# The second stage's projection steps on TensorE, issued in four pieces between the attention's products

## The chip, the cores and the metric

The kernel runs on one core of one Trainium2 chip. The core has five engines that run their own instruction streams and meet at semaphores: TensorE (PE in the rows; PEld is its weight load), VectorE (DVE), ScalarE (ACT), GpSimd (POOL) and SyncE (SP), which issues the DMAs. The metric is the time on the device in microseconds (us), the median of several runs.

## The reference, cut to what matters

Two transformer layers over four batches of 512 tokens of width 256. The change concerns the end of the first layer's attention and the projections of the second layer:

```
xn = layernorm(x)
# layer 0: 16 heads of 16
scores = einsum('bhqd,bhkd->bhqk', q, k) * scale
attn = einsum('bhqk,bhkd->bhqd', softmax(scores), v)
combined = g * mem_out / denom + (1 - g) * attn
x = x + combined @ Wo.T + ffn0(xn)
# layer 1
xn = layernorm(x)
q, k, v = silu(xn @ Wq), silu(xn @ Wk), silu(xn @ Wv)
gate = (xn @ Wg1) @ Wg2
logits = xn @ w_router          # two experts of eight per token
```

What follows (the linear attention of layer 1, its experts and the sum) is the third stage.

## The kernel before, in words

There are three stages, with a barrier between them. The first normalises, projects q, k, v of layer 0 and runs its experts; the second, the function `middle`, does the softmax attention of layer 0 and, beside it, the projections of layer 1; the third does the rest.

The second stage goes through four batches, each in four groups of four heads, each group in four tiles of 128 keys: sixteen tiles a batch, here 0 to 15, which the code calls slots. In one tile TensorE makes, for each of the four heads h, a score product (line 1219, into `psE`, two buffers in turn) and a row product (line 1201, into `psM`, two buffers in turn). The score products are of the present group; ScalarE turns each into probabilities with an exponential (line 1006). The row products are of the group after the next; VectorE takes from each the negated maximum of a row (line 1075), which the scores of that group will need. Then `values` (line 1228) multiplies the four heads' probabilities of the tile before with v, four matmuls of 32 output rows. Once in a group, in its second tile, four small transposes (line 1208) turn the maxima of the next group; VectorE copies them (line 1098) and two DMAs bring them into place.

Beside the attention of batch n + 1 run the steps of batch n, each in a fixed tile and, on every engine, after that engine's own attention work of the tile (`beside`). On TensorE: heads 0 to 3 in tiles 0 to 3 (lines 1267, 1270), the transposes of the combined heads in 4, the output projection in 5, the transposes of x in 8, the first half projection (q) in 9, the router's logits and the low-rank gate input in 10, its transposes in 11, the second half (k) in 12, the gate in 13, k by tokens in 14 and v by tokens in 15. The other engines' steps between them: VectorE combines the terms (`weigh_terms`, 0 to 3), adds the residual, normalises (7), splits x into a high and a low part (8), chooses the experts (10); ScalarE copies (4, 8) and applies Silu or a sigmoid (9, 12 to 15), for which it loads another activation table and then the exponential's again; GpSimd adds the terms. A TensorE step waits at its first matmul for the other engine's step on its input, and hands on at its last matmul. The first batch has nothing beside it; the last batch's own steps come at the end, alone.

All instructions of an engine run in the order in which they are written; semaphores make them wait. In `attend` that order, within a tile, is: two scores, (the turned maxima,) two rows, the values of the tile before, two scores, the whole step, two rows.

Of the kernel before, what the change touches and what calls it, by code (L numbers as in the profile page):

```python
# [732 lines left out]
RW = E + HD  # L733
# [3 lines left out]
def middle(nc, io, scratch, keep):  # L737
# [8 lines left out]
    with ExitStack() as ctx:  # L746
# [12 lines left out]
        ident, identb = sb("ident", [P, P]), sb("identb", [P, P], BF16)  # L759
# [67 lines left out]
        STORES, PARTS = 16 * STORES1, 16 * PARTS1  # L827
        SLOTS = GROUPS * TILES

        def loop(eng, attend, steps, ready=lambda: None):  # L830


            def batch(b, beside, last):
                for g in range(GROUPS):
                    attend(b, g, last, lambda k: [step(beside) for step in steps.get(TILES * g + k, ()) if beside is not None])

            batch(0, None, False)
            ready()
            with eng.Fori(0, BATCHES - 2) as b:
                batch(b + 1, b, False)  # L840
            batch(BATCHES - 1, BATCHES - 2, True)
            for slot in sorted(steps):
                for step in steps[slot]:
                    step(BATCHES - 1)
# [349 lines left out]
        def _(pe):  # L1194
# [17 lines left out]
            def attend(b, g, last, beside):  # L1212
# [20 lines left out]
                for k in range(TILES):  # L1233
                    ahead = not (last and g >= GROUPS - 2)
                    next_rows = G + 2, (g + 2) % GROUPS, k, b if g < 2 else b + 1
                    scores(k, (0, 1))
                    if k == 1 and not (last and g == GROUPS - 1):
                        turn_max(G + 1, (g + 1) % 2)
                    if ahead:
                        rows(*next_rows, (0, 1))  # L1240
                    if k:
                        values(k - 1)
                    scores(k, (2, 3))
                    beside(k)
                    if ahead:
                        rows(*next_rows, (2, 3))
                values(TILES - 1)


            def heads(t):  # L1250
                def step(n):

                    if t == 0:
                        pe.wait_ge(out_copied, GROUPS * (n + 1))
                        pe.wait_ge(qf_in, 16 * n + 16)
                        pe.wait_ge(v_done, n)
                    elif not alone(n):
                        pe.wait_ge(terms, TILES * n + t)
                    elif t == 1:
# [6 lines left out]
                    for g in range(GROUPS):  # L1266
                        nc.tensor.matmul(ps[:, 0, g * w:(g + 1) * w], outT[:, g, c], sel[:, :], start=True, stop=True,
                                         skip_group_check=True)
                    for k in range(KT):
# [3 lines left out]
                    mm.then_inc(heads_ps, 1)  # L1273
                return step

            def turn_combined(n):
                pe.wait_ge(combined_done, TILES * n + TILES)
                for t in range(TILES):
                    for k in range(KT):
                        mm = nc.tensor.transpose(psX[:, k, t * P:(t + 1) * P], combined[:, t, k * P:(k + 1) * P], ident[:, :])  # L1280
                mm.then_inc(combT_ps, 1)

            def project_out(n):
                pe.wait_ge(combT_done, n + 1)
                for t in range(TILES):
                    for k in range(KT):
                        mm = nc.tensor.matmul(psX[:, t // 2, t % 2 * D:(t % 2 + 1) * D], combT[:, k, t * P:(t + 1) * P], wo[:, k, :],
                                              start=k == 0, stop=k == KT - 1, skip_group_check=True)
                mm.then_inc(y_ps, 1)

            def turn_x(n):
                pe.wait_ge(norm.xn_done, TILES * n + TILES)
                for t in range(TILES):
                    for k in range(KT):
                        mm = nc.tensor.transpose(psX[:, k, t * P:(t + 1) * P], xn[:, t, k * P:(k + 1) * P], ident[:, :])
                mm.then_inc(xT_ps, 1)

            def project_half(i):
                def step(n):
                    if i == 0:  # L1300
                        pe.wait_ge(xlo, n + 1)
                    elif not alone(n):
                        pe.wait_ge(lowT_done, n + 1)
                        pe.wait_ge(routing.copied, n + 1)
                    else:
# [8 lines left out]
            def logits_low(n):  # L1314
                if not alone(n):
                    pe.wait_ge(half_done, 2 * n + 1)
                for t in range(TILES):
                    c = slice(t * P, (t + 1) * P)
                    mm = three(nc, second(n)[:, 0, t * RW:(t + 1) * RW],
                               [(xT[0][:, k, c], xT[1][:, k, c], wr[0][:, k, :], wr[1][:, k, :]) for k in range(KT)])  # L1320
                mm.then_inc(low_ps, 1)

            def turn_low(n):
                pe.wait_ge(low_done, n + 1)
                for t in range(TILES):
                    mm = nc.tensor.transpose(second(n)[0:HD, 1, t * P:(t + 1) * P], low[:, t, :], ident[:, :])
                mm.then_inc(lowT_ps, 1)

            def project_gate(n):
                pe.wait_ge(lowT_done, n + 1)  # L1330
                pe.wait_ge(routing.copied, n + 1)
                if not alone(n):
                    pe.wait_ge(half_done, 2 * n + 2)
                for t in range(TILES):
                    mm = nc.tensor.matmul(second(n)[:, t // 2, (t % 2) * D:(t % 2 + 1) * D], lowT[:, t * P:(t + 1) * P],
                                          wg2[:, :], start=True, stop=True, skip_group_check=True)
                mm.then_inc(gate_ps, 1)

            def project_tokens(i, free, done):

                def step(n):
                    ps = second(n) if i else psX
                    if not alone(n):
                        pe.wait_ge(free, n + 1)
                    elif i:
                        pe.wait_ge(gate_done, n + 1)
                    else:
                        pe.wait_ge(half_done, 2 * n + 2)
                    for t in range(TILES):
                        c = slice(t * P, (t + 1) * P)  # L1350
                        mm = three(nc, ps[:, t // 2, (t % 2) * D:(t % 2 + 1) * D],
                                   [(xT[0][:, k, c], xT[1][:, k, c], wkv[0][:, k, i * D:(i + 1) * D], wkv[1][:, k, i * D:(i + 1) * D])
                                    for k in range(KT)])
                    mm.then_inc(done, 1)
                return step

            for t in range(TILES):
# [8 lines left out]
            def ready():  # L1366
# [694 lines left out]
```

## Time and profile before

| | us |
|---|---|
| median of 3 runs | 1190.88 (1188.92 to 1192.23) |
| profiled execution, span of its instructions | 1186.0 |
| second stage, first row product to the end of its last steps | 309 to about 730 |
| TensorE busy, share of the span | 972.0 (82%) |
| VectorE busy | 584.5 (49%) |
| ScalarE busy | 433.3 (37%) |
| GpSimd busy | 311.8 (26%) |

Times of the trace are counted from the span's start. The profile has no time of the profiled execution beyond its span; the runs' median is 4.9 us longer than that span. Matmuls are pipelined, so that the duration of one overlaps the next: distances from start to start tell what a group of matmuls costs. A granted clock of 1.00 is 2.4 GHz, 0.50 is 1.2 GHz, and a value between is the mean of a stretch that has both.

### The profile page before, as it was taken

Reading aid. Unit: us, or ns where it says so; the run is one execution under the profiler, and the core shown is the slowest. Engines: PE = TensorE matmul, PEld = TensorE weight load, DVE = VectorE, ACT = ScalarE, POOL = GpSimd, SP = SyncE. Lnnn points to the kernel's source line nnn. Section 1 sums busy time; section 2 is a strip of 40 time slices with the busy share of each in tenths; the row PEclk is TensorE's granted clock in tenths of the full one; section 3 lists DMA queues with packets and bytes.
Section 4 is the critical chain, followed back from the end, with each engine's and each line's share of the span. In section 5 each row is a group of like instructions: output and inputs, shape, how many; then the busy total and the mean of one; then the engine's idle time right before and its main releaser. Section 6 shows DMA issues by size and latency. Waiting matters only on the chain. (4 is left out here: it accounts for less than half of the span.)

```text
span 1186.0 us, 16176 instructions
## 1 busy us (share of the span) xinstructions
PE 972.0 (82%) x5323; PEld 623.9 (53%) x5323; DVE 584.5 (49%) x1221; ACT 433.3 (37%) x662; POOL 311.8 (26%) x217
## 2 busy tenths in 40 slices
PE   3699999999589999999998763259999888999871
PEld 2588888888112334444434552235556555665541
DVE  4556566643577785577573322533233333333335
ACT  3435354452245556647646513002222221222210
POOL 3622425153230002012002121033333333333210
PEclk9989999999679998899898877569999999999975
DMA  6713314240523222412321205994322232333352
GB/s 212 224 36 96 110 54 150 54 151 1 145 62 91 66 79 93 145 59 89 133 65 63 98 32 165 274 286 122 109 77 80 80 77 76 85 78 89 81 175 71
DMA packets 150413, 125.47 MB, mean 106 GB/s; under 512 B 63424, under 2 KB 128080, under 8 KB 150352
## 3 DMA queue, kind: packets, MB, share of 16 engines
q1 hardware_dynamic: 146608, 114.45, 32.4%
q0 software_dynamic: 3744, 10.23, 2.9%
q8 instruction: 36, 0.59, 0.2%
q14 instruction: 25, 0.20, 0.1%
HBM read 85.76 MB, written 38.86 MB: 105 GB/s over the span
## 5 line engine op out<-in xcount | busy, mean ns | idle before, releaser
L1075 DVE TENSOR_REDUCE b_negmax<-b_psM 128x1 f32<-128x512 f32 x256 | 163.2, 683 | 75.6 <-PE b_psM L1201 72.6
L1006 ACT ACTIVATE b_probs<-b_psE 128x512 f32<-128x512 f32 x256 | 138.8, 595 | 118.2 <-PE b_psE L1219 117.3
L1201 PE MATMUL b_psM<-b_kst,b_qst 96*128 96x512 bf16 x256 | 98.5, 432 | 27.6 <-DVE b_negmax L1075 13.7
L1219 PE MATMUL b_psE<-b_qst,b_kst 98*128 98x512 bf16 x256 | 89.8, 410 | 15.4 <-ACT b_probs L1006 10.8
L402 POOL TENSOR_TENSOR a_hh<-a_h,a_hh 128x512 fp32r<-128x512 f32 x44 | 57.7, 1312 | 145.5 <-ACT a_hh L455 145.5
L1580 POOL DMA_INDIRECT scratch_ys<-d_y,d_put x39 | 40.2, 1030 | 178.4 <-ACT d_y L1618 176.8
L1847 PE MATMUL d_psG<-d_w,d_xT 128*128 x156 | 80.7, 642 | 4.1 <-issue 3.2
L1855 PE MATMUL d_psU<-d_w,d_xT 128*128 x156 | 79.9, 638 | 0.0
L1219 PEld LDWEIGHTS b_psE<-b_qst,b_kst 98*128 98x128 bf16 x256 | 20.9, 99 | 107.4 <-ACT b_probs L1006 53.8
L1872 PE MATMUL d_psY<-d_w,d_hidden 128*128 x312 | 76.7, 390 | 0.3 <-ACT d_hidden L1612 0.3
L1228 PE MATMUL b_psV<-b_probs,b_vst 128*32 128x512 f32 x512 | 73.6, 648 | 3.2 <-ACT b_probs L1006 3.2
L1586 POOL TENSOR_TENSOR d_rs<-d_ss,d_neghalf 128x16 f32<-128x16 f32 x16 | 46.8, 2928 | 93.0 <-DVE d_ss L1762 93.0
L1201 PEld LDWEIGHTS b_psM<-b_kst,b_qst 96*128 96x128 bf16 x256 | 24.3, 100 | 84.0 <-DVE b_negmax L1075 60.5
L1872 PEld LDWEIGHTS d_psY<-d_w,d_hidden 128*128 128x128 f32 x312 | 58.7, 194 | 15.5 <-issue 8.9
L1732 DVE TENSOR_TENSOR d_probs<-d_ps,decay 128x512 f32<-128x512 f32 x64 | 43.2, 687 | 43.4 <-PE d_ps L1886 43.1
L528 DVE TENSOR_TENSOR a_h<-a_h,a_psG 128x512 f32<-128x512 f32 x44 | 30.2, 686 | 68.4 <-ACT a_h L452 68.4
L1618 ACT ACTIVATE d_y<-d_psY 128x256 f32<-128x256 f32 x39 | 14.9, 383 | 125.4 <-PE d_psY L1872 125.4
L1727 DVE TENSOR_TENSOR d_hidden<-d_hidden,d_psU 128x512 f32<-128x512 f32 x39 | 26.8, 687 | 67.2 <-PE d_psU L1855 67.0
L1931 PE MATMUL d_ps<-d_ident,d_normed 128*128 128x128 f32 x32 | 8.0, 337 | 61.6 <-DVE d_normed L1770 61.6
L1606 ACT ACTIVATE d_hidden<-d_psG 128x512 f32<-128x512 f32 x39 | 23.3, 597 | 94.2 <-PE d_psG L1847 94.2
L956 POOL TENSOR_TENSOR b_combined<-b_both 128x256 f32<-128x256 f32 x16 | 11.6, 724 | 167.6 <-DVE b_both L1119 167.6
L455 ACT ACTIVATE a_hh<-a_h 128x512 fp32r<-128x512 f32 x44 | 27.8, 632 | 73.7 <-DVE a_h L533 73.7
(310 smaller groups left out, 2174.7 us busy)
## 6 DMA issues: line engine op xcount, KB each, us to landing
scratch_parts<-a_part SPq DMA_DIRECT2D x12, 512.0 KB, 4.0
b_qst<-scratch_parts SPq DMA_DIRECT2D x96, 64.0 KB, 2.3
b_kst<-scratch_parts SPq DMA_DIRECT2D x96, 64.0 KB, 2.3
scratch_parts<-b_part SPq DMA_DIRECT2D x24, 256.0 KB, 3.4
d_qst<-scratch_parts SPq DMA_DIRECT2D x96, 64.0 KB, 2.7
d_kst<-scratch_parts SPq DMA_DIRECT2D x96, 64.0 KB, 2.9
a_cbc<-scratch_cT SPq DMA_DIRECT2D x16, 256.0 KB, 3.9
scratch_v<-a_v SPq DMA_DIRECT2D x4, 1024.0 KB, 4.3
```

The costliest lines, as they stand in the source:

```text
L402: nc.gpsimd.tensor_tensor(hh[s % HSLOTS][1][:, :], h[s % 2][:, :], hh[s % HSLOTS][0][:, :].bitcast(F32), ALU.subtract).then_inc(lo_done, 1)
L1006: nc.scalar.activation(probs[k % PSLOTS][:, h, :], psE[h % 2][:, :], ACT.Exp, scale=float(HD) ** -0.5).then_inc(scores_used[h % 2], 1)
L1075: nc.vector.tensor_reduce(negmax[i][:, t, h:h + 1], psM[:, h % 2, :], AX_X, ALU.max, negate=True).then_inc(rows_used[h % 2], 1)
L1201: nc.tensor.matmul(psM[:, h % 2, :], qst[g][0:STACK, h, t * P:(t + 1) * P], kst[g][0:STACK, h, :], start=True, stop=True).then_inc(rows_re ...
L1219: nc.tensor.matmul(psE[h % 2][:, :], kst[g][0:STACKM, h, k * P:(k + 1) * P], qst[g][0:STACKM, h, :], start=True, stop=True).then_inc(score ...
L1228: mm = nc.tensor.matmul(psV[VW * h:VW * (h + 1), :], vst[g][:, k, VW * h:VW * (h + 1)], probs[k % PSLOTS][:, h, :], start=k == 0, stop=k = ...
L1580: nc.gpsimd.indirect_dma_start(scratch["ys1"], bass.IndirectOffsetOnAxis(ap=put[:, b:b + 1], axis=0), y[b % YSLOTS][:, :], None).then_inc( ...
L1586: nc.gpsimd.tensor_tensor(rs[:, :], ss[:, :], neghalf[:, :], ALU.pow).then_inc(rs_done, 1)
L1732: nc.vector.tensor_tensor(probs[g][:, :], (ps1 if g % 2 else ps0)[:, :], decay[:, HG * g:HG * g + HG, :].rearrange("p h c -> p (h c)"), AL ...
L1847: mm = nc.tensor.matmul(psG[:, :], xT[b % 2][:, k, :], weights(b, GATE + k * H1, H1), start=k == 0, stop=k == KT - 1)
L1855: mm = nc.tensor.matmul(psU[:, :], xT[b % 2][:, k, :], weights(b, UP + k * H1, H1), start=k == 0, stop=k == KT - 1)
L1872: mm = nc.tensor.matmul(psY[:, 0:D], hT[b % 2][:, k, :], weights(b, DOWN + k * D, D), start=k == 0, stop=k == HT1 - 1)
```

## The change

Each of TensorE's steps is cut into four pieces of equal work (a quarter of its matmuls in the same order), and the four heads of a tile are no longer taken in pairs: behind the score of each head come its row product and then one piece of the step. The values of the tile before come behind the second piece. The waits of a step stand before its first piece, and its hand-over after its last piece, as they stood before its first and after its last matmul. The steps keep their tiles, and the other engines their order. In the batch at the end, without attention beside it, the pieces follow each other and the order is that of before.

```diff
                 for k in range(TILES):
                     ahead = not (last and g >= GROUPS - 2)
                     next_rows = G + 2, (g + 2) % GROUPS, k, b if g < 2 else b + 1
-                    scores(k, (0, 1))
-                    if k == 1 and not (last and g == GROUPS - 1):
-                        turn_max(G + 1, (g + 1) % 2)
-                    if ahead:
-                        rows(*next_rows, (0, 1))
-                    if k:
-                        values(k - 1)
-                    scores(k, (2, 3))
-                    beside(k)
-                    if ahead:
-                        rows(*next_rows, (2, 3))
+                    for h in range(HG):
+                        scores(k, (h,))
+                        if ahead:
+                            rows(*next_rows, (h,))
+                        if k == 1 and h == 0 and not (last and g == GROUPS - 1):
+                            turn_max(G + 1, (g + 1) % 2)
+                        beside(k, h)
+                        if k and h == 1:
+                            values(k - 1)
                 values(TILES - 1)
...
             def project_half(i):
-                def step(n):
-                    if i == 0:
+                def step(n, piece):
+                    if piece == 0 and i == 0:
                         pe.wait_ge(xlo, n + 1)
-                    elif not alone(n):
+                    elif piece == 0 and not alone(n):
                         pe.wait_ge(lowT_done, n + 1)
                         pe.wait_ge(routing.copied, n + 1)
-                    else:
+                    elif piece == 0:
                         pe.wait_ge(half_done, 2 * n + 1)
-                    for m in range(KT):
-                        c = slice((KT * i + m) * P, (KT * i + m + 1) * P)
-                        mm = three(nc, psX[:, m, :], [(wqk[0][:, k, c], wqk[1][:, k, c], xT[0][:, k, :], xT[1][:, k, :])
-                                                      for k in range(KT)])
-                    mm.then_inc(half_ps, 1)
+                    m, k = piece // KT, piece % KT
+                    c = slice((KT * i + m) * P, (KT * i + m + 1) * P)
+                    mm = three(nc, psX[:, m, :], [(wqk[0][:, k, c], wqk[1][:, k, c], xT[0][:, k, :], xT[1][:, k, :])],
+                               start=k == 0, last=k == KT - 1)
+                    if piece == KT * KT - 1:
+                        mm.then_inc(half_ps, 1)
                 return step
...
             loop(pe, attend, {0: (heads(0),), 1: (heads(1),), 2: (heads(2),), 3: (heads(3),), 4: (turn_combined,), 5: (project_out,),
                               8: (turn_x,), 9: (project_half(0),), 10: (logits_low,), 11: (turn_low,), 12: (project_half(1),),
                               13: (project_gate,), 14: (project_tokens(0, gate_done, kk_ps),),
-                              15: (project_tokens(1, kk_done, v_ps),)}, ready)
+                              15: (project_tokens(1, kk_done, v_ps),)}, ready, tuple((piece,) for piece in range(HG)))
```

On TensorE, a tile of the first batch, with nothing beside it (`b_psE` are scores, `b_psM` rows, `b_psV` values), before:

```order
L1219 MATMUL b_psE<-b_qst,b_kst 128x512 x2
L1201 MATMUL b_psM<-b_kst,b_qst 128x512 x2
L1228 MATMUL b_psV<-b_probs,b_vst 32x512 x4
L1219 MATMUL b_psE<-b_qst,b_kst 128x512 x2
L1201 MATMUL b_psM<-b_kst,b_qst 128x512 x2
```

and the same tile now:

```order
L1220 MATMUL b_psE<-b_qst,b_kst 128x512
L1202 MATMUL b_psM<-b_kst,b_qst 128x512
L1220 MATMUL b_psE<-b_qst,b_kst 128x512
L1202 MATMUL b_psM<-b_kst,b_qst 128x512
L1229 MATMUL b_psV<-b_probs,b_vst 32x512 x4
L1220 MATMUL b_psE<-b_qst,b_kst 128x512
L1202 MATMUL b_psM<-b_kst,b_qst 128x512
L1220 MATMUL b_psE<-b_qst,b_kst 128x512
L1202 MATMUL b_psM<-b_kst,b_qst 128x512
```

Each row product stands behind its own head's score. On TensorE, tile 2 with heads 2 beside it (`b_psX`, from `b_outT` and from `mem`), before:

```order
L1219 MATMUL b_psE<-b_qst,b_kst 128x512 x2
L1201 MATMUL b_psM<-b_kst,b_qst 128x512 x2
L1228 MATMUL b_psV<-b_probs,b_vst 32x512 x4
L1219 MATMUL b_psE<-b_qst,b_kst 128x512 x2
L1267 MATMUL b_psX<-b_sel,b_outT 128x68 x4
L1270 MATMUL b_psX<-mem,b_qf 128x136 x2
L1201 MATMUL b_psM<-b_kst,b_qst 128x512 x2
```

and the same tile now:

```order
L1220 MATMUL b_psE<-b_qst,b_kst 128x512
L1202 MATMUL b_psM<-b_kst,b_qst 128x512
L1267 MATMUL b_psX<-b_sel,b_outT 128x68 x2
L1220 MATMUL b_psE<-b_qst,b_kst 128x512
L1202 MATMUL b_psM<-b_kst,b_qst 128x512
L1267 MATMUL b_psX<-b_sel,b_outT 128x68 x2
L1229 MATMUL b_psV<-b_probs,b_vst 32x512 x4
L1220 MATMUL b_psE<-b_qst,b_kst 128x512
L1202 MATMUL b_psM<-b_kst,b_qst 128x512
L1271 MATMUL b_psX<-mem,b_qf 128x136
L1220 MATMUL b_psE<-b_qst,b_kst 128x512
L1202 MATMUL b_psM<-b_kst,b_qst 128x512
```

The step's first matmul moved from behind the fourth score to behind the first row, and its last from ahead of the third row to behind the fourth.

## Rows read from the trace of the kernel before

**Rows 1.** Waits, 330 to 700 us: who waited for whom, total us, times, longest

```profile
ACT b_probs L1006 <- PE b_psE L1219: 117.3, 74, 4.2
DVE b_negmax L1075 <- PE b_psM L1201: 72.6, 41, 4.5
```

**Rows 2.** Four batches: us, busy (x count) of each engine, granted clock, DMA share, GB/s

```profile
331.70:401.50 69.80, 60.78 (x291) 16.05 (x292) 52.94 (x86) 38.16 (x69) 4.87 (x3) 0.91 0.26 75
401.50:496.10 94.60, 87.61 (x461) 42.53 (x460) 62.28 (x135) 56.66 (x84) 12.66 (x9) 0.92 0.25 79
496.10:587.60 91.50, 84.76 (x461) 40.11 (x460) 62.97 (x135) 56.67 (x84) 12.66 (x9) 0.95 0.31 103
587.60:673.50 85.90, 75.24 (x406) 37.63 (x404) 40.70 (x95) 53.06 (x79) 12.63 (x9) 0.91 0.25 83
```

**Rows 3.** Order of time, first batch: start, us, engine, line, out<-in [idle before <-releaser]

```profile
378.76 1.07 PE L1228 MATMUL b_psV<-b_probs,b_vst 128*32 128x512 f32 x8
379.76 0.60 PE L1219 MATMUL b_psE<-b_qst,b_kst 98*128 98x512 bf16 x2
380.20 0.60 PE L1201 MATMUL b_psM<-b_kst,b_qst 96*128 96x512 bf16 x2
...
377.09 2.64 DVE L1075 TENSOR_REDUCE b_negmax<-b_psM 128x1 f32<-128x512 f32 x4 [0.89 <-PE b_psM L1201]
```

**Rows 4.** Order of time, TensorE, heads in tiles 1 and 2

```profile
404.82 1.01 PE L1267 MATMUL b_psX<-b_sel,b_outT 128*128 128x68 f32 x8
...
406.18 0.60 PE L1201 MATMUL b_psM<-b_kst,b_qst 96*128 96x512 bf16 x2
...
411.06 0.60 PE L1201 MATMUL b_psM<-b_kst,b_qst 96*128 96x512 bf16 x2
```

**Rows 5.** Order of time, VectorE, tile 1: reductions, combining, next reductions

```profile
406.60 1.29 DVE L1075 TENSOR_REDUCE b_negmax<-b_psM 128x1 f32<-128x512 f32 x2 [0.86 <-PE b_psM L1201]
407.81 0.35 DVE L1114 RECIPROCAL b_scale<-b_psX 128x32 f32<-128x32 f32 x1
...
409.02 1.28 DVE L1075 TENSOR_REDUCE b_negmax<-b_psM 128x1 f32<-128x512 f32 x2
```

**Rows 6.** Order of time, tiles 8 and 9: copy, split, half projection, rows

```profile
440.69 1.02 ACT L1017 ACTIVATE b_xT<-b_psX 128x1024 fp32r<-128x1024 f32 x1 [0.28 <-PE b_psX L1295]
442.68 1.20 DVE L1138 TENSOR_TENSOR b_xT<-b_psX,b_xT 128x1024 fp32r<-128x1024 f32 x1
443.94 0.19 PEld L58 LDWEIGHTS b_psX<-b_xT,b_wqk 128*128 128x128 f32 x1
443.96 0.59 PE L58 MATMUL b_psX<-b_xT,b_wqk 128*128 128x512 f32 x1
444.38 0.40 PE L59 MATMUL b_psX<-b_xT,b_wqk 128*128 128x512 f32 x1
...
446.89 0.61 PE L1201 MATMUL b_psM<-b_kst,b_qst 96*128 96x512 bf16 x2
```

**Rows 7.** Order of time, ScalarE, tile 9: table load and Silu

```profile
445.23 1.28 ACT L1023 ACT_TABLE_LOAD   x1
447.08 1.02 ACT L1023 ACTIVATE b_half<-b_psX 128x1024 f32<-128x1024 f32 x1 [0.57 <-PE b_psX L60]
```

**Rows 8.** Order of time, VectorE and TensorE at the turn of the batch

```profile
489.91 1.22 DVE L1158 TENSOR_TENSOR b_part<-b_half,b_part 128x1024 bf16<-128x1024 f32 x1
491.04 1.22 DVE L1142 TENSOR_TENSOR b_kd<-b_combT,b_kdec 128x1024 f32<-128x1024 f32 x1
...
492.48 0.69 DVE L1105 COPY b_outT<-b_psV 128x512 f32<-128x512 f32 x1
...
493.47 1.41 PE L1267 MATMUL b_psX<-b_sel,b_outT 128*128 128x68 f32 x8 [0.63 <-DVE b_outT L1105]
```

**Rows 9.** Stretches of 2 us, columns as in rows 2

```profile
366.00:368.00 2.00, 1.38 (x11) 0.31 (x11) 1.72 (x5) 0.62 (x2) 0.00 (x0) 1.00 0.04 13
...
454.00:456.00 2.00, 2.00 (x6) 0.51 (x4) 1.59 (x5) 0.85 (x2) 0.73 (x1) 0.50 0.00 0
...
586.00:588.00 2.00, 2.00 (x10) 1.39 (x9) 0.55 (x2) 0.00 (x0) 0.00 (x0) 0.56 0.47 142
```

More of the change, by code:

```diff
@@ L828, in middle, with loop @@
         SLOTS = GROUPS * TILES
-        def loop(eng, attend, steps, ready=lambda: None):
+        def loop(eng, attend, steps, ready=lambda: None, pieces=((),)):
             def batch(b, beside, last):
                 for g in range(GROUPS):
-                    attend(b, g, last, lambda k: [step(beside) for step in steps.get(TILES * g + k, ()) if beside is not None])
+                    attend(b, g, last, lambda k, *piece: [step(beside, *piece) for step in steps.get(TILES * g + k, ()) if beside is not None])
             batch(0, None, False)
@@ L843, in loop @@
                 for step in steps[slot]:
-                    step(BATCHES - 1)
+                    for piece in pieces:
+                        step(BATCHES - 1, *piece)
         def alone(n):
@@ L1265, in step @@
                     c, w = slice(t * P, (t + 1) * P), HG * (HD + 1)
[L1266 to L1269, printed above, removed]
+                    if piece < 2:
+                        for g in (2 * piece, 2 * piece + 1):
+                            nc.tensor.matmul(ps[:, 0, g * w:(g + 1) * w], outT[:, g, c], sel[:, :], start=True, stop=True,
+                                             skip_group_check=True)
+                    else:
+                        k = piece - 2
                         mm = nc.tensor.matmul(ps[:, 1, MW * k:MW * (k + 1)], qf[:, k, c],
@@ L1283, in project_out @@
[L1283 to L1296, printed above, removed]
+                        if k == KT - 1:
+                            mm.then_inc(heads_ps, 1)
@@ L1316, in logits_low @@
+                return step
+            def logits_low(n, t):
+                if t == 0 and not alone(n):
                     pe.wait_ge(half_done, 2 * n + 1)
-                for t in range(TILES):
-                    c = slice(t * P, (t + 1) * P)
[L1319 to L1354, printed above, removed]
+                c = slice(t * P, (t + 1) * P)
@@ new lines, in logits_low, with turn_low @@
+                mm = three(nc, second(n)[:, 0, t * RW:(t + 1) * RW],
+                           [(xT[0][:, k, c], xT[1][:, k, c], wr[0][:, k, :], wr[1][:, k, :]) for k in range(KT)])
+                if t == TILES - 1:
+                    mm.then_inc(low_ps, 1)
+            def turn_low(n, t):
+                if t == 0:
+                    pe.wait_ge(low_done, n + 1)
+                mm = nc.tensor.transpose(second(n)[0:HD, 1, t * P:(t + 1) * P], low[:, t, :], ident[:, :])
+                if t == TILES - 1:
+                    mm.then_inc(lowT_ps, 1)
@@ new lines, in project_gate @@
+            def project_gate(n, t):
+                if t == 0:
+                    pe.wait_ge(lowT_done, n + 1)
+                    pe.wait_ge(routing.copied, n + 1)
+                if t == 0 and not alone(n):
+                    pe.wait_ge(half_done, 2 * n + 2)
+                mm = nc.tensor.matmul(second(n)[:, t // 2, (t % 2) * D:(t % 2 + 1) * D], lowT[:, t * P:(t + 1) * P],
+                                      wg2[:, :], start=True, stop=True, skip_group_check=True)
+                if t == TILES - 1:
+                    mm.then_inc(gate_ps, 1)
@@ new lines, in project_tokens, with step @@
+            def project_tokens(i, free, done):
+                def step(n, t):
+                    ps = second(n) if i else psX
+                    if t == 0 and not alone(n):
+                        pe.wait_ge(free, n + 1)
+                    elif t == 0 and i:
+                        pe.wait_ge(gate_done, n + 1)
+                    elif t == 0:
+                        pe.wait_ge(half_done, 2 * n + 2)
+                    c = slice(t * P, (t + 1) * P)
+                    mm = three(nc, ps[:, t // 2, (t % 2) * D:(t % 2 + 1) * D],
+                               [(xT[0][:, k, c], xT[1][:, k, c], wkv[0][:, k, i * D:(i + 1) * D], wkv[1][:, k, i * D:(i + 1) * D])
+                                for k in range(KT)])
+                    if t == TILES - 1:
+                        mm.then_inc(done, 1)
```

41 lines of the change are left out of this document (27 added, 14 removed).

## The prediction

> **What bounds the kernel now.** I read the stretches of the second stage first, then its waits, then TensorE's, VectorE's and ScalarE's instructions in order of time in the batch that begins at 401.5 us. Name the products of one tile s (score), r (row), V (values) and b (the step beside); number the sixteen tiles of a batch 0 to 15; call the start of a tile's fourth row product its mark. From mark to mark the first batch, which has no step beside it, takes 69.8 us with its start-up, the next two 94.6 and 91.5, and the last, to the end of its values, 85.9 [rows 2]. In these three TensorE is busy 93, 93 and 88%, VectorE 66, 69 and 47%, ScalarE about 61%: TensorE's row of instructions is the path. ScalarE and VectorE wait for it, 117.3 us for scores and 72.6 us for rows [rows 1], because a whole step (1.36 us for heads, 2.93 us for a half projection) stands between two pairs of products [rows 4, 6].
>
> The granted clock is part of that length. 0.92, 0.95 and 0.91 are means of the two levels, so 2 x (1 - clock) x length = 15.1, 9.2 and 15.5 us pass at 1.2 GHz; at 2.4 GHz that work takes half. Without these stretches the three batches are 94.6 - 7.6 = 87.0, 91.5 - 4.6 = 86.9 and 85.9 - 7.7 = 78.2 us. The first two, which do the same work, agree to 0.1 us, so I hold the slow stretches to be on the path.
>
> **Batch 0: two products closer.** Here only the order of s, r and V changes. Before, VectorE does four reductions in 2.64 us and waits 0.89 us: a tile is 3.52 us [rows 3]. The limit is a ring: r1 waits for the reduction of r3 of the tile before, then V (1.0 us) and s2, s3 (0.44) come before r2. After, r2 and r3 have one score between them and s2 alone ahead: from a mark, the reduction of r3 ends at +1.2; r1 can start at +1.27, ends at +1.5, V at +2.5, s2, r2, s3 (0.22 each) at +3.16. That is 0.36 us less in two tiles of four; the second tile of a group gains 0.2 and the first 0.1 in the same way. 1.0 us a group, four groups: **-4.0 us**.
>
> **The steps: the wait comes 1.9 us sooner.** Each step waits, at its first matmul, for another engine's work on the step before, and that work is queued behind that engine's four exponentials or reductions of the tile before. Before, TensorE had r2, r3, s0, s1, r0, r1, V, s2, s3 (2.9 us) to issue in the meantime; now it has r3, b3, s0, r0. What stands behind the waiting matmul is everything TensorE has: s1 and r1, on which ScalarE and VectorE then run dry. So a tile becomes release + 3 pieces + s1, r1, V, s2, r2, s3 = release + 3 pieces + 2.1 us, from mark to mark, where the release is counted from the last mark.
>
> Tiles 2 and 3 (heads): r3's reduction starts 0.42 after the mark and ends at 1.03; the combining of the terms takes 1.21 us (407.81 to 409.02) [rows 5]; release 2.33 with the signal. A piece is 1.36 / 4 = 0.34. 2.33 + 1.05 + 2.1 = 5.48, before 4.88 [rows 4]. Tile 1 has the turned maxima and their copy ahead of the combining: 6.25. Three tiles: 17.2.
>
> Tiles 9, 10, 13, 14 and 15 wait for a ScalarE step. Tile 9: s3's exponential ends at 0.75, the copy of 1.02 us at 1.8, VectorE's split of 1.20 us at 3.05 [rows 6]. Tile 10: exponential 0.75, table load 1.28 us, Silu 1.02 us, 3.05 [rows 7]. The other three have the same load and a 1024-wide activation. TensorE reaches its wait at 1.1 to 1.35, so it stands about 1.8 us. A piece of 2.93 us less the 0.2 of its first load is 0.68 [rows 6]: 3.1 + 2.04 + 2.1 = 7.24, five tiles 36.2. (The gate's pieces are shorter and the token projections' longer; together they differ by 0.3.)
>
> Tile 0 of the next batch waits for the last copy of outT. VectorE has, behind r3's reduction at 1.03, two passes of 1.2 us, the split maxima and a copy of 0.69 us [rows 8]: release 4.45, three pieces, and s1, r1, s2, r2, s3 without V: 6.6 us. Before, TensorE waited there 0.63 us, with s2, s3, r0 and r1 already out.
>
> Tiles 4 to 8, 11 and 12, walked in the same way: 4.9 (GpSimd's sum of the terms is the release), 6.6, 3.72, 4.35, 4.78 (VectorE's normalisation is), 4.52 and 5.38. They sum to 34.3; VectorE's own work sets most of them, and the spread rows help it.
>
> A batch is 17.2 + 36.2 + 6.6 + 34.3 = 94.3 us at full clock, against 87.0 and 86.9: +7.3 and +7.4. In the last batch groups 2 and 3 have no rows, so a tile there is 0.44 us shorter (6.8 five times, 3.6, 3.25, 4.7, and 1.95 to the end of V: 47.5); with 17.2 and 19.6 for tiles 1 to 7 it is 84.3, against 78.2: +6.1. Together **+20.8 us**. The last batch's steps, done with nothing beside them, keep their order: 0.
>
> **The first weight load of a step.** The 0.19 us load of the half projection's first matmul begins at 443.94, just after the split's end at 443.88 [rows 6]: it starts behind its wait and not before, and the second matmul starts 0.42 us after the first, where a product of 512 columns takes 0.22. Most steps of before waited for nothing and paid little of it; now about eight in a batch do: 8 x 0.19 x 3 = **+4.6 us**, between 0 and this. The Trainium skill, in "TensorE: Matmul & The Clock Gate" (section "What a matmul computes"), says that weight loads are pulled ahead of running matmuls; were that so across the wait too, this term would be 0 and the sum 4.6 less. The row shows it otherwise.
>
> **The clock.** It falls to 0.50 after the narrow matmuls of the logits (454 to 456), and to 0.56 behind the pauses at the turn of a batch (586 to 588) [rows 9]. The change removes long narrow stretches, since the logits come in quarters, and adds pauses. No row shows both together. Bounds: all 39.8 us of slow stretches go, -19.9 us; or they double, +19.9 us. I take the number of today, 0 change, midway between the two and nearest to the rows.
>
> **Sum.** -4.0 + 20.8 + 4.6 = +21.4 us on the profiled execution, whose span is 1186.0 us: 1207.4. The runs' median of 1190.88 is 4.9 above that span, so **1212 us**, with 1200 to 1226 as its own range (the load term 0, two microseconds either way in each batch's walk, and some of the clock).
>
> **Rivals.**
> *More pauses, more time at 1.2 GHz.* The slow stretches double: 1212 + 19.9 = 1232 us. For it: about nine waits in a batch of 1.3 to 2 us, and the pauses at the turn of a batch were followed by a fall [rows 9]. Against it: at 366 to 368, in the first batch, TensorE was busy 1.38 of 2 us, and the clock stayed at 1.00 [rows 9]. The Trainium skill has this as a rule ("TensorE: Matmul & The Clock Gate", section "A second HAM failure mode: psum-queue depth-cycling"): short idle moments between groups of matmuls let the clock swing between its levels. The row at 586 agrees; the row at 366 does not.
>
> *The clock stays up.* With the logits in quarters no slow stretch is left: 1212 - 19.9 = 1192 us, no measurable change. For it: the longest falls follow logits and gate. Against it: the pause at each of these steps.
>
> *The waits are covered, and it is faster.* If the releasing steps end before TensorE comes to the first piece, the batch is TensorE's work: 5.5 us in place of 7.24 in five tiles, 4.3 in place of 5.7 in three, 3.2 in place of 6.6 at the turn of the batch, some 15 us less than 94.3, or 8 less than 87. Three batches and the first: about -24 - 4, 1163 us. It decides at the first piece: 21.4 us over 27 waits (nine a batch) is 0.8 each, so where the waits average under 1.0 us instead of 1.8 the change is not slower. For it: VectorE and ScalarE wait 190 us for TensorE, and both are fed more evenly. Against it: s3's exponential, an activation of 1.02 us and a table load all follow the fourth score, and only 1.1 to 1.35 us of TensorE's work cover them.
>
> **How the numbers follow.** Forecast 0.56, more slow clock 0.20, clock stays up 0.12, covered 0.12. About 0.3% (3.6 us) is what a measurement of this kernel tells from no change. Covered is faster; the case at 1192 I split into 0.03 faster, 0.05 same, 0.04 slower; the rest is slower: 0.15, 0.05, 0.80. The range goes from 1190, which takes in the case of the steady clock, to 1236; it leaves out the covered case and the worst clock.
>
> **What would show it.** Waits of TensorE's first piece, in the half and token projections for ScalarE or VectorE, of 1.5 to 2 us each; the heads' matmuls waiting over 1 us for the combining; batches of 94 to 101 us; a first batch 4 us shorter, its VectorE waiting less for rows. Wrong would be: these waits under 1 us, batches under 90 us, or a mean clock above 0.97 in the three.

## The result, and the profile after

The change made the kernel slower: 1241.44 us (median of 4 runs, 1239.57 to 1242.45) against 1191.56 us for the kernel before, run beside it, a ratio of 1.041 with a 95% interval of 1.0388 to 1.0433. The forecast was 1212 us with a range up to 1236: the direction was right, the size too small by 29 us.

First where the time went. The same stretches as in [rows 2], from mark to mark, in the kernel after; in front of them the first batch from its first row product to the first heads matmul, 87.04 us, where before the same stretch is 91.03 us. Columns as in [rows 2]. The first batch before:

```profile
308.87:399.90 91.03, 78.52 (x315) 18.12 (x315) 73.82 (x121) 46.54 (x93) 9.36 (x4) 0.81 0.34 96
```

After:

```profile
312.38:399.42 87.04, 76.65 (x311) 18.25 (x311) 71.30 (x120) 45.73 (x90) 9.34 (x4) 0.80 0.33 97
...
402.30:512.80 110.50, 91.78 (x462) 46.10 (x460) 67.27 (x136) 59.43 (x85) 12.66 (x9) 0.87 0.23 70
512.80:626.40 113.60, 96.24 (x462) 46.84 (x460) 65.52 (x136) 59.30 (x84) 12.67 (x9) 0.82 0.25 82
626.40:725.60 99.20, 81.29 (x404) 40.20 (x402) 41.90 (x94) 54.14 (x78) 12.65 (x9) 0.84 0.21 71
```

The three batches are 110.50, 113.60 and 99.20 us against 94.60, 91.50 and 85.90: +51.3 us. The granted clock, next to last but two, fell to 0.87, 0.82 and 0.84. Worked as in the prediction, 2 x (1 - clock) x length, 28.7, 40.9 and 31.7 us passed at 1.2 GHz, 101.3 us in place of 39.8. Half of the difference is 30.8 us; what is left, 20.5 us, is length at full clock: 96.1, 93.2 and 83.3 us against 87.0, 86.9 and 78.2. The span as a whole grew by 54.7 us (1186.0 to 1240.7): counted from heads to heads the three batches give +53.0, the first batch -4.0, the first stage +3.5 (its end moved from 308.87 to 312.38, with no change in its code) and all behind the batches +2.2. The medians grew by less, 49.9 us. In every run that lists both, the time is 1.75 to 1.85 us above the span (1242.45 and 1240.7 here), so the profiled execution of before was nearly 4 us faster than its median, and that of after 1 us slower than its own.

Who waits now. First for TensorE, as in [rows 1], over 330 to 760 us (the batches are longer); then TensorE's own waits between 395 and 690 us, before and after (the last batch ends at 674 us before and at 727 after, so that the list of after lacks a third of it). Columns: who waited for whom, total us, times, longest.

```profile
ACT b_probs L1007 <- PE b_psE L1220: 176.3, 148, 4.2
DVE b_negmax L1076 <- PE b_psM L1202: 101.0, 87, 3.3
```

Before:

```profile
PE b_psE L1219 <- ACT b_probs L1006: 10.8, 11, 1.6
PE b_psM L1201 <- DVE b_negmax L1075: 7.0, 28, 0.6
PE b_psX L1280 <- POOL b_combined L956: 3.2, 4, 2.4
PE b_psX L1267 <- DVE b_outT L1105: 1.4, 2, 0.8
```

After:

```profile
PE b_psX L1267 <- DVE b_both L1120: 13.3, 9, 1.8
PE b_psX L58 <- DVE b_xT L1139: 5.5, 3, 2.1
PE b_psX L58 <- ACT b_half L1024: 5.4, 3, 2.1
PE b_psX L1267 <- DVE b_outT L1106: 4.1, 3, 1.9
...
PE b_psX L58 <- ACT b_sg L1042: 3.4, 2, 1.9
PE b_psX L58 <- ACT b_combT L1047: 3.3, 2, 1.6
```

ScalarE waited 117.3 us for scores before and waits 176.3 now, VectorE 72.6 and now 101.0: both starve behind a TensorE that stands at the first piece of a step. Those waits (`b_psX`) were nearly absent before. In the three whole batches of after, the nine tiles that the prediction named have 27 of them, 43 us together: 0.45 us at the very first and 1.3 to 2.2 us at the other 26.

One of them from near by: TensorE in order of time, tiles 1 and 2 with heads beside them (start, us, engine, line, out<-in, and in brackets the idle time before and what ended it).

```profile
404.76 0.81 PE L1267 MATMUL b_psX<-b_sel,b_outT 128*128 128x68 f32 x4 [1.79 <-DVE b_both L1120]
405.36 0.64 PE L1220 MATMUL b_psE<-b_qst,b_kst 98*128 98x512 bf16 x1
405.79 0.64 PE L1202 MATMUL b_psM<-b_kst,b_qst 96*128 96x512 bf16 x1
406.21 0.96 PE L1267 MATMUL b_psX<-b_sel,b_outT 128*128 128x68 f32 x4
...
409.69 0.38 PE L1202 MATMUL b_psM<-b_kst,b_qst 96*128 96x512 bf16 x1
...
412.07 0.66 PE L1267 MATMUL b_psX<-b_sel,b_outT 128*128 128x68 f32 x4 [1.33 <-DVE b_both L1120]
412.57 0.38 PE L1220 MATMUL b_psE<-b_qst,b_kst 98*128 98x512 bf16 x1
412.79 0.38 PE L1202 MATMUL b_psM<-b_kst,b_qst 96*128 96x512 bf16 x1
...
415.39 0.38 PE L1202 MATMUL b_psM<-b_kst,b_qst 96*128 96x512 bf16 x1
```

From mark (409.69) to mark (415.39) tile 2 takes 5.70 us, where the prediction's walk through the tile had 5.48, and its release comes 2.38 us after the mark, where the walk had 2.33. That is the wait's own price. The other price stands in the lines behind 404.76: after the wait of 1.79 us a score and its row are 0.43 us apart (405.36 to 405.79), after the wait of 1.33 us 0.22 (412.57 to 412.79). The granted clock beside it, in stretches of 2 us, columns as before:

```profile
406.00:408.00 2.00, 2.00 (x13) 1.09 (x12) 0.69 (x1) 0.60 (x1) 0.00 (x0) 0.50 0.52 138
...
412.00:414.00 2.00, 1.93 (x18) 1.36 (x18) 1.31 (x3) 0.60 (x1) 0.72 (x1) 1.00 0.00 0
...
450.00:452.00 2.00, 2.00 (x7) 1.18 (x5) 0.64 (x1) 0.60 (x1) 0.00 (x0) 0.50 0.56 166
...
488.00:490.00 2.00, 1.78 (x7) 1.53 (x8) 0.78 (x2) 1.97 (x3) 0.00 (x1) 0.50 0.46 159
...
508.00:510.00 2.00, 2.00 (x9) 1.53 (x9) 0.69 (x1) 0.60 (x1) 0.00 (x0) 0.50 0.44 130
```

At 450, 488 and 508 it is the same: 0.50 right behind a first piece that waited, 1.70 us at the half projection, 1.93 at the token projection, 1.91 at the turn of the batch.

Over the three batches of after the trace has 15 separate stretches at 0.50. Fourteen begin within 2.5 us of the end of one of the 26 long waits, and one (at 487.1 us) inside the wait that ends at 488.22. Of the other 11 waits three end in a stretch that was already at 0.50, and eight bring no fall, such as that of 1.33 us at 412.07.

### The profile page after: what moved, and what is told of

Read it like the earlier page. It is cut to its first block and busy times, and to the rows that moved or that the text cites. A ratio compares the mean times of both kernels' runs of the same rounds, so it can differ in the third digit from the quotient of the medians.

```text
span 1240.7 us, 16176 instructions
## 1 busy us (share of the span) xinstructions
PE 997.2 (80%) x5323; PEld 642.7 (52%) x5323; DVE 593.5 (48%) x1221; ACT 441.7 (36%) x662; POOL 311.8 (25%) x217
## 5 line engine op out<-in xcount | busy, mean ns | idle before, releaser
L1076 DVE TENSOR_REDUCE b_negmax<-b_psM 128x1 f32<-128x512 f32 x256 | 167.5, 685 | 103.1 <-PE b_psM L1202 101.0
L1007 ACT ACTIVATE b_probs<-b_psE 128x512 f32<-128x512 f32 x256 | 148.5, 597 | 178.9 <-PE b_psE L1220 176.3
L1202 PE MATMUL b_psM<-b_kst,b_qst 96*128 96x512 bf16 x256 | 114.0, 447 | 22.0 <-DMA b_vst<-scratch_v 11.3
L1220 PE MATMUL b_psE<-b_qst,b_kst 98*128 98x512 bf16 x256 | 110.2, 431 | 0.5
L1229 PE MATMUL b_psV<-b_probs,b_vst 128*32 128x512 f32 x512 | 82.0, 716 | 5.8 <-ACT b_probs L1007 5.6
L1220 PEld LDWEIGHTS b_psE<-b_qst,b_kst 98*128 98x128 bf16 x256 | 27.1, 106 | 88.9 <-issue 75.9
L455 ACT ACTIVATE a_hh<-a_h 128x512 fp32r<-128x512 f32 x44 | 27.8, 633 | 73.7 <-DVE a_h L533 73.7
```

What stands on the lines that cost most here:

```text
L1007: nc.scalar.activation(probs[k % PSLOTS][:, h, :], psE[h % 2][:, :], ACT.Exp, scale=float(HD) ** -0.5).then_inc(scores_used[h % 2], 1)
L1076: nc.vector.tensor_reduce(negmax[i][:, t, h:h + 1], psM[:, h % 2, :], AX_X, ALU.max, negate=True).then_inc(rows_used[h % 2], 1)
L1202: nc.tensor.matmul(psM[:, h % 2, :], qst[g][0:STACK, h, t * P:(t + 1) * P], kst[g][0:STACK, h, :], start=True, stop=True).then_inc(rows_re ...
L1220: nc.tensor.matmul(psE[h % 2][:, :], kst[g][0:STACKM, h, k * P:(k + 1) * P], qst[g][0:STACKM, h, :], start=True, stop=True).then_inc(score ...
L1229: mm = nc.tensor.matmul(psV[VW * h:VW * (h + 1), :], vst[g][:, k, VW * h:VW * (h + 1)], probs[k % PSLOTS][:, h, :], start=k == 0, stop=k = ...
```

## The experiments

In each profile I measured the three batches with a step beside them from heads to heads (before: 399.90 to 674.30 us), and worked out the time at 1.2 GHz from the clock of each batch's row; "at full clock" is the length less half of that time. The clock has two digits, which makes an error of about 1 us of slow time a batch. Time in which TensorE stands idle is counted with the rest, though a slow clock costs nothing there: it is 5.8 us of the slow time after and 1.1 before, so that half of the slow time is good to 2 or 3 us. Each ratio is to runs of the kernel before beside it, whose medians were 1191.56, 1193.24 and 1192.67 us.

| kernel | median us | ratio to before (95%) | three batches | of it at 1.2 GHz | at full clock |
|---|---|---|---|---|---|
| before | 1191.56 | 1 | 274.4 | 41.9 | 253.4 |
| after | 1241.44 | 1.041 (1.0388 to 1.0433) | 327.4 | 100.9 | 277.0 |
| rows alone | 1199.91 | 1.0049 (1.0021 to 1.0078) | 279.7 | 37.1 | 261.2 |
| pieces alone | 1272.92 | 1.0665 (1.0626 to 1.0704) | 356.6 | 133.1 | 290.0 |
| pieces late | 1196.08 | 1.002 (0.9992 to 1.0047) | 282.6 | 54.4 | 255.4 |
| after, nine waits filled | 1211.38 | 1.0125 (1.0077 to 1.0173) | 299.9 | 27.8 | 286.0 |
| after, heads filled | 1227.35 | 1.0296 (1.0263 to 1.0329) | 313.1 | 69.2 | 278.5 |
| after, the rest filled | 1217.46 | 1.0193 (1.0157 to 1.023) | 309.0 | 47.5 | 285.2 |
| first batch alone | 1191.15 | 0.9979 (0.9961 to 0.9998) | 278.6 | 51.9 | 252.7 |
| pieces from the middle | 1177.07 | 0.9881 (0.9848 to 0.9914) | 263.8 | 27.8 | 249.9 |

My theory (W in the first expectations): what costs is that a step's first piece stands at its wait sooner, and the pauses bring TensorE's clock down.

**Rows alone.** Behind the fourth score the whole step, as before; each row behind its own score.

```diff
+ for h in range(HG):
+     scores(k, (h,))
+     if h == 3:
+         for piece in range(HG):
+             beside(k, piece)
+     if ahead:
+         rows(*next_rows, (h,))
...
```

> Only the order of the products is the changed kernel's: each row product behind its own head's score. The step stands whole behind the fourth score, as before. Theory W (the steps' waits come too early, and the pauses bring the clock down): no step waits earlier than before, so the first batch keeps its gain of 2.7 us and the three others lose nothing: 1183 to 1190 us, slow clock in them near the 40 us of before. Rival A (single products in alternation cost by themselves, on TensorE or on the engines behind it): most of the loss stays, above 1225 us.

Measured 1199.91 us, ratio 1.0049, outside the expected 1183 to 1190. The 50 us don't come from the rows' order: the steps' waits are not there. But it is not the gain I expected either, and the two largest of TensorE's waits between 395 and 690 us, which were 7.0 and 10.8 us before, say where it is lost:

```profile
PE b_psM L1202 <- DVE b_negmax L1076: 17.5, 18, 2.0
PE b_psE L1220 <- ACT b_probs L1007: 13.6, 17, 1.6
```

With a step in one lump, the spread rows are a loss of 8 us at full clock in the three batches, which was no term of my sum. The profile is of the fastest of the ten runs (1189.67 us, mean granted clock 0.898; the others are 1194 to 1206 us at 0.883 to 0.895), so it shows the place of the loss and not all of it.

**Pieces alone.** One piece behind each score, the rows in pairs as before.

```diff
- scores(k, (0, 1))
+ scores(k, (0,))
...
+ beside(k, 0)
+ scores(k, (1,))
+ beside(k, 1)
...
```

> Only the cut of the steps is the changed kernel's: one piece behind each score, the row products in pairs at the places of before. Theory W: the first piece now has one product less ahead of it than in the changed kernel, so its waits are as long or 0.2 us longer: 1235 to 1260 us, 80 us or more of slow clock in the three batches. Rival A: with the rows in pairs the loss goes, under 1205 us.

Measured 1272.92 us, more than the whole change and above my range. The first piece now stands behind a single score, and its waits are longer still. TensorE's two largest waits, same stretch:

```profile
PE b_psX L1274 <- DVE b_both L1120: 18.4, 9, 2.2
PE b_psX L1274 <- DVE b_outT L1106: 6.9, 3, 3.2
```

Nine waits of 18.4 us in place of 13.3, three of 6.9 in place of 4.1, and 133.1 us at 1.2 GHz in place of 100.9. So the loss is in the pieces' places and not in the rows' order; that a row more in front of each first piece hides some of it is what the longer waits suggest.

**Pieces late.** The four pieces stay pieces, two behind head 2's row and two behind head 3's.

```diff
- beside(k, h)
+ if h >= 2:
+     beside(k, 2 * h - 4)
+     beside(k, 2 * h - 3)
```

> The changed kernel with the pieces later in the tile: two behind the third head's products, two behind the fourth's, so that the first piece has the values and four more products ahead of it (2.3 us more cover). Theory W: the waits of 1.3 to 2 us vanish and with them the slow clock they bring: 1180 to 1195 us. A rival, C: the steps' cut into pieces and more changes of operand bring the clock down, whatever the waits: 1215 us or more with waits under 0.5 us.

Measured 1196.08 us, ratio 1.002 with 1 in its interval: no difference that can be told. Its 54.4 us at 1.2 GHz are near the 51.9 us of a kernel whose three batches have the code of before (first batch alone, below), so the rival of this run, that cut steps bring the clock down whatever the waits, falls. Cutting the steps costs nothing that these runs can see; starting them sooner does. TensorE's waits for `b_both` are gone from its list, and for `b_outT` one of 0.8 us is left.

**Nine waits filled.** This one is to tell the clock's part from the waits' part. The changed kernel gets work that nobody needs, in front of the first piece in tiles 0 to 3, 9, 10 and 13 to 15: six matmuls of 512 columns whose result nothing reads.

```diff
+ if piece == 0 and not alone(n):
...
+     for _ in range(6):
+         nc.tensor.matmul(psNf[64:P, :], kst[g][0:STACK, 0, 0:64], qst[g][0:STACK, 0, :],
+                          start=True, stop=True, tile_position=(0, 64), skip_group_check=True)
```

> The changed kernel, with six added matmuls of 512 columns (about 1.3 us at 2.4 GHz), whose result nothing reads, ahead of the first piece in the nine tiles where it waits 1.3 to 2 us. They fill most of the pause and leave the waits' ends where they are. Theory W with its clock part: the slow clock of 101 us in the three batches falls to 40 us or less, and half of the difference is saved: 1205 to 1220 us. Rival D (the slow stretches lie beside the waits and cost nothing, the waits alone are the loss): the clock rises and the time stays at 1236 to 1245 us. Where the clock does not rise, this run tells nothing between the two.

Measured 1211.38 us: 30 us less than the changed kernel, with some 1.4 us of added work at 27 places. Its batches, heads to heads, and the first filled wait:

```profile
396.13:496.83 100.70, 92.88 (x516) 45.31 (x515) 67.12 (x135) 58.62 (x85) 12.71 (x9) 0.98 0.24 73
496.83:597.25 100.42, 92.73 (x514) 45.47 (x514) 67.48 (x136) 58.78 (x84) 12.66 (x9) 0.98 0.29 94
597.25:696.01 98.76, 90.81 (x471) 45.73 (x471) 45.15 (x98) 57.81 (x84) 12.67 (x9) 0.90 0.23 77
```

```profile
399.65 1.48 PE L1255 MATMUL b_psN<-b_qst,b_kst 96*64 96x512 bf16 x6
401.51 0.66 PE L1278 MATMUL b_psX<-b_sel,b_outT 128*128 128x68 f32 x4 [0.38 <-DVE b_both L1121]
402.01 0.38 PE L1221 MATMUL b_psE<-b_qst,b_kst 98*128 98x512 bf16 x1
402.23 0.38 PE L1203 MATMUL b_psM<-b_kst,b_qst 96*128 96x512 bf16 x1
```

The wait of 1.79 us in tile 1 is 0.38 now, the piece comes no sooner (its release is VectorE's), and the products behind it are 0.22 apart, not 0.43. In the first two batches the clock is 0.98. At full clock the three are no shorter, 286.0 us against 277.0. Part of the 9 us between are TensorE's waits for VectorE's reductions, after and here:

```profile
PE b_psM L1202 <- DVE b_negmax L1076: 3.7, 7, 0.8
```

```profile
PE b_psM L1203 <- DVE b_negmax L1077: 7.9, 8, 2.4
```

Another part are idle matmuls that last beyond the release: some 38 us of them took 36 us off the first pieces' waits. The rest is within the 2 or 3 us of the halves. Less slow clock, 100.9 to 27.8 us, gives 36.6 us; less the 9.0 that is 27.6, the three profiled batches' difference, and the medians differ by 30. The clock's part of the loss is shown by this run and not only worked out. The logits in quarters pass at full clock in its first two batches; the one fall in each (0.86 from 462 to 474 and from 562 to 574 us, 1.00 elsewhere) comes behind a wait of 2.41 us for those reductions.

**Heads filled, and the rest filled.** The same idle matmuls, in tiles 0 to 3 alone, and in tiles 9, 10 and 13 to 15 alone.

```diff
- for slot in (0, 1, 2, 3, 9, 10, 13, 14, 15):
+ for slot in (0, 1, 2, 3):                      # heads filled
+ for slot in (9, 10, 13, 14, 15):               # the rest filled
```

> The changed kernel with six idle matmuls of 512 columns, whose result nothing reads, ahead of the first piece in tiles 0 to 3 alone (four of the nine long waits of a batch). With them ahead of all nine waits the time came down by 30 us. If each wait brings its share of slow clock: 4/9 of 30 us come back, 1225 to 1232 us. Rival (the slow clock comes from the projections' waits in tiles 9 to 15): 1238 us or more. Rival (the falls feed each other, and breaking the row of waits at one place is enough): 1218 us or less.

> The changed kernel with the same six idle matmuls ahead of the first piece in tiles 9, 10, 13, 14 and 15 alone (the other five of the nine long waits). If each wait brings its share of slow clock: 5/9 of 30 us come back, 1220 to 1228 us. Rival (the slow clock comes from the heads' waits in tiles 0 to 3): 1236 us or more. Rival (the falls feed each other): 1218 us or less, with the tiles 0 to 3 at full clock too.

Measured 1227.35 us, 14 us back, in the stretch of the equal shares; and 1217.46 us, 24 us back, a little more than its share. That lies under the 1218 us of the rival too, by which the falls feed each other; the rival also wanted the tiles 0 to 3 at full clock, and they are so in one of the two batches below. So these two runs do not settle the rival. Neither place alone is the cause and neither alone is enough. The granted clock by stretches shows where it is up: the first heads, then tiles 9 to 12 of the same batch (with the end of tile 8), then the heads of the next batch; columns as before. Heads filled:

```profile
399.32:420.00 20.68, 20.30 (x125) 11.54 (x124) 13.31 (x25) 8.85 (x16) 2.17 (x3) 1.00 0.16 46
...
442.00:478.00 36.00, 30.98 (x141) 15.12 (x140) 22.16 (x49) 19.59 (x29) 6.61 (x3) 0.81 0.21 65
...
505.79:526.00 20.21, 19.83 (x122) 11.25 (x123) 13.22 (x25) 8.86 (x15) 2.17 (x3) 1.00 0.46 161
```

The rest filled:

```profile
398.53:418.00 19.47, 15.02 (x100) 8.97 (x101) 12.85 (x24) 8.67 (x15) 2.17 (x3) 1.00 0.19 56
...
440.00:475.00 35.00, 31.36 (x162) 14.75 (x154) 23.83 (x52) 18.93 (x28) 6.61 (x3) 0.90 0.23 70
...
500.74:522.00 21.26, 16.81 (x85) 9.81 (x86) 12.20 (x23) 7.67 (x13) 2.05 (x3) 0.76 0.44 153
```

Where the waits are filled beside heads, the clock is 1.00 in both batches, and 0.81 in the tiles 9 to 12, whose waits are open. With the rest filled these tiles have 0.90 and the heads of the second batch 0.76. The first line of the last fence is the exception: heads with their waits of 1.79 and twice 1.33 us open, and the clock stayed at 1.00. The two gains sum to 38 us where both together give 30, so the shares don't simply add.

**First batch alone.** The kernel before, with the alternating order only in the batch that has no step beside it.

```diff
+ if isinstance(b, int) and b == 0:
+     for h in range(HG):
+         scores(k, (h,))
+         rows(*next_rows, (h,))
...
```

> The kernel before with one part of the change alone: in the first batch, which has no step beside it, each row product stands behind its own head's score; the other three batches keep the order of before. My term for this was -4.0 us, and the batch was 4.0 us shorter in the changed kernel: 1187 to 1190 us where the kernel before has 1191 to 1193, a ratio of 0.996 to 0.998. Rival (the batch ends sooner but the second batch then waits for a transfer or starts at a lower clock): a ratio of 0.999 or more.

Measured a ratio of 0.9979 (0.9961 to 0.9998), a gain of 2.5 us with an interval from 0.2 to 4.7: in the range of ratios expected, though the median of 1191.15 us is above the 1187 to 1190, and under my term of 4.0. The interval reaches into the rival's range (0.999 or more). In its profile the first batch took 88.67 us; over the eight profiles with this order it is 86.70 to 88.67, 87.7 in the mean, against 91.03 in before's profile. In pieces alone, whose first batch has before's order but for one tile in four, it is 88.99, so that a single profile of this batch is good to about two microseconds.

**Pieces from the middle.** Theory W also says what to do: keep the pieces, and put the first where its release is near. First piece behind the second row and the values, second behind the third row, the last two behind the fourth.

```diff
- beside(k, h)
  if k and h == 1:
      values(k - 1)
+ if h == 1:
+     beside(k, 0)
+ if h == 2:
+     beside(k, 1)
+ if h == 3:
+     beside(k, 2)
+     beside(k, 3)
```

> The changed kernel with its first piece moved from behind the first row product to behind the second row product and the values; the second piece goes behind the third row product and the last two behind the fourth. In front of each step's first matmul there are then a score, a row and the values (1.44 us) more than in the change, so the waits of 1.3 to 1.9 us should shrink to 0.5 us or less. Theory (what costs is the length of the wait, and most of it through the clock): batches of 92 to 98 us, the mean granted clock in the three at 0.91 or more, 1190 to 1207 us. Rival (any wait at a step's first matmul brings the clock down, however short): clock at 0.86 or less as in the change, 1220 us or more.

Measured 1177.07 us (1176.72 to 1180.77), ratio 0.9881 (0.9848 to 0.9914): faster than both kernels, and below the stretch I gave. Its batches, heads to heads, and the first pieces of tiles 1 and 9:

```profile
397.54:487.81 90.27, 81.34 (x461) 40.96 (x461) 63.81 (x136) 59.05 (x86) 12.69 (x9) 0.96 0.26 81
487.81:577.82 90.01, 81.49 (x462) 41.66 (x463) 65.08 (x136) 58.51 (x85) 12.65 (x9) 0.96 0.32 106
577.82:661.36 83.54, 75.39 (x420) 38.48 (x419) 43.49 (x98) 56.60 (x83) 12.64 (x9) 0.92 0.27 91
```

```profile
403.06 0.66 PE L1273 MATMUL b_psX<-b_sel,b_outT 128*128 128x68 f32 x4 [0.26 <-DVE b_both L1120]
...
441.00 0.50 PE L58 MATMUL b_psX<-b_xT,b_wqk 128*128 128x512 f32 x1 [0.17 <-DVE b_xT L1139]
```

Waits of 1.79 and 1.70 us became 0.26 and 0.17, and in tiles 2 and 3 none is left. The longest wait for a step's input in its three batches is 0.8 us. Of the 63.6 us by which the three batches are shorter than the changed kernel's, 27.1 are length at full clock (277.0 to 249.9) and 36.6 half of the slow time (100.9 to 27.8).

## Why the prediction was wrong

*What bounds: right.* TensorE's row of instructions is the path; idle matmuls, which raise its busy time, shortened the kernel only through the clock.

*Batch 0, -4.0 us: right in sign, a little large.* The one profile gives -4.0, the timed run of this part alone -2.5 (0.2 to 4.7). A profile of this batch is good to about 2 us, so how much too large stays open.

*The steps' waits, +20.8 us: right.* The waits stand where they were to stand, with the length that was worked out (release 2.38 us after the mark in tile 2 against 2.33; 1.70 at the half projection and 1.93 at a token projection against about 1.8; 1.6 in the mean of all 27). At full clock the three batches grew by 20.5 us.

*The first weight load, +4.6 us: too large, from a line read wrongly.* The prediction took the 0.42 us from the first matmul of the half projection to its second as one product of 0.22 us and the price of the load. The line of before that stands in front of them says otherwise:

```profile
443.70 0.60 PE L1219 MATMUL b_psE<-b_qst,b_kst 98*128 98x512 bf16 x2
```

These two scores begin at 443.70 and 0.22 us later, so that from 443.70 to 444.38 there are three products in 0.68 us, and the load cost nothing there. Where TensorE does stand at the wait, in the changed kernel, the load again begins with the end of the wait, and the second matmul starts 0.33 us after the first:

```profile
449.12 0.19 PEld L58 LDWEIGHTS b_psX<-b_xT,b_wqk 128*128 128x128 f32 x1 [1.89 <-DVE b_xT L1139]
449.12 0.50 PE L58 MATMUL b_psX<-b_xT,b_wqk 128*128 128x512 f32 x1 [1.70 <-DVE b_xT L1139]
449.45 0.57 PE L59 MATMUL b_psX<-b_xT,b_wqk 128*128 128x512 f32 x1
```

That is 0.1 us for a wait and not 0.19; for 27 waits it would be 2.7 us, an estimate from this one place. Tile 2 agrees, 3.32 us from its release to its mark (412.07 to 415.39) where three pieces and the products are 3.15. The sum doesn't show it: waits and loads together are 20.5 us, not 25.4, so other tiles are shorter than I walked them, and I did not find which.

The Trainium skill says ("TensorE: Matmul & The Clock Gate", section "Step-by-step: what each phase is for"; the prediction names another section of that page) that weight loads are pulled ahead of running matmuls. In this trace that does not reach past the load's own wait, as the load at 449.12 shows.

*The clock, 0 us: this is the step that failed.* I put it "midway between the two" bounds of -19.9 and +19.9. It was +30.8 us by marks, outside both, since slow time went up by a factor of 2.5 and not 2. Two errors are in it. I let the narrow matmuls of the logits stand for the cause, as a fall of before followed them [rows 9], and so reckoned that quartering them might give time back; the nine waits a batch, which I had counted and priced, I did not carry into this term. And I took the stretch at 366 us [rows 9], busy 1.38 of 2 us at a clock of 1.00, as evidence against: its idle time is one pause of 0.62 us in front of the values, and the waits that I had worked out are two to three times that long. The bound "they double" was a round number and no bound. One from the waits would have been wide enough: 27 of them, each followed by a slow stretch such as the one from 405.36 to 408.80 in the changed kernel (3.4 us, half of it lost), are 46 us.

With the clock term at +30.8 in place of 0 the sum is 21.4 + 30.8 = 52.2 us on the profiled execution, less 4.9 for the load term that the total doesn't show, plus 5.7 for the stages before and behind; the span grew by 54.7. (The 1.7 us left are there because the three batches grew by 51.3 us from mark to mark and by 53.0 from heads to heads.)

*The rivals.* "More pauses, more time at 1.2 GHz" was the right mechanism, and had 0.20 and a price that was too low. The Trainium skill's rule beside it ("TensorE: Matmul & The Clock Gate", section "A second HAM failure mode: psum-queue depth-cycling") speaks of this: short idle moments between groups of matmuls let the clock swing. Here the trace agrees, and shows a price: 59 us more at 1.2 GHz in the three batches (41.9 to 100.9), and 30 us of time given back by filling the moments. "The clock stays up" fell with 0.87, 0.82 and 0.84. "Waits covered" fell with the waits of 1.3 to 2.2 us (its three terms make 16 us a batch and not 15, so that its price was nearer 1160 than 1163 us), but its condition was right: the run with the first piece in the middle, whose waits for a step's input are 0.8 us at most, is faster than before, by 1.2%.

## What to carry to other kernels

Cutting a long step into pieces helps the engines that it starves only if its first piece still stands where its input is ready: put the first piece by the release, counted in work that the engine has left to issue, and let the others follow. When a change adds pauses to TensorE, price each twice, once as idle time and once as the slow clock that may follow, and don't take a neutral value for the second because the signs are unknown. Idle matmuls in the pauses are a quick test that tells the two apart.

## What the runs showed of the hardware that I had not expected

More work made the kernel faster: six idle matmuls in each of nine waits a batch took it from 1241.44 to 1211.38 us, through 73 us less at 1.2 GHz.

The same pause does not always bring the clock down. In the changed kernel the heads' wait of 1.79 us at 404.76 was followed by 0.50; in the kernel with the rest filled the same wait in the same tile (and two of 1.33 us behind it) by 1.00. In the changed kernel's three batches 14 of 26 long waits were followed by a fall. What makes the difference I did not find, so that a count of pauses gives a likely price and not a sure one. In kernels with the same code in these three batches (before, and first batch alone) the slow time was 41.9 and 51.9 us, which is 5 us of the kernel's time. The spread from run to run goes the same way: of 19 runs of the kernel before, the fastest, 1187.34 us, has a mean granted clock of 0.895, and the slowest, 1197.73 us, 0.881.
